# A perceiver layer on one core: GpSimd takes nine of the low halves, the first pass ends in finer steps, and feature products change place

## The reference, cut to what matters

```python
Sim = (encoder_hc @ w1)[:, :, None] + (decoder_hq @ w2)[:, None, :] \
    + jnp.einsum('bid,bjd->bij', encoder_hc * w3, decoder_hq) + b_sim[0]
A = jax.nn.softmax(Sim, axis=2)
hq_hat = jnp.einsum('bij,bjd->bid', A, decoder_hq)
Batt = jax.nn.softmax(jnp.max(Sim, axis=2), axis=1)
hc_bar = jnp.einsum('bi,bid->bd', Batt, encoder_hc)[:, None, :]
hc_hat = jnp.broadcast_to(hc_bar, encoder_hc.shape)
feats = jnp.concatenate([encoder_hc, hq_hat, encoder_hc * hq_hat, encoder_hc * hc_hat], axis=-1)
hcq = feats @ W_qv + b_qv
```

## Time and profile before

| | us |
|---|---|
| three runs, median (lowest to highest) | 124.64 (123.28 to 125.08) |
| the profiled execution, device time | 122.58 |
| its span in the profile | 120.7 |
| first pass, first scores to last scores on PE | 6.3 to 43.3 |
| first exponential | 45.1 |
| first mix to last mix | 48.4 to 97.2 |
| tail | 97.2 to 120.7 |
| DMA traffic | 29.27 MB, at about 410 GB/s until 72 us |

### The profile page before, as it was taken

How to read it: one execution, slowest core, us unless ns; L and a number is a source line. 1 busy time by engine, 2 the same in 40 slices (tenths; PEclk the granted TensorE clock), 3 DMA queues, 4 the chain that set the end, 5 groups by cost and what they waited for, 6 DMA issues and landing times.

```text
span 120.7 us, 1711 instructions
## 1 busy us (share of the span) xinstructions
PE 111.7 (93%) x569; PEld 84.6 (70%) x569; DVE 93.5 (77%) x140; ACT 69.0 (57%) x118; POOL 23.9 (20%) x35
## 2 busy tenths in 40 slices
PE   6789999999999995999999999999999969999890
PEld 2237675858685872888898879899898947665280
DVE  1549999999999989799999964899999533271442
ACT  4075758467473209997998844988887530221220
POOL 2100000000003420327755502353540001000100
PEclk9999999999999999999999999999999999999999
DMA  3999999999999999999999994300000000000001
GB/s 85 347 406 415 413 411 406 410 411 406 413 407 408 410 414 404 411 413 433 385 414 407 408 334 181 87 5 0 0 0 0 5 0 0 0 0 0 3 0 43
DMA packets 8073, 29.27 MB, mean 242 GB/s; under 512 B 1025, under 2 KB 1281, under 8 KB 7810
## 3 DMA queue, kind: packets, MB, share of 16 engines
q1 hardware_dynamic: 7920, 29.17, 61.6%
q10 hardware_dynamic: 146, 0.01, 0.1%
HBM read 29.04 MB, written 0.13 MB: 242 GB/s over the span
## 4 chain that ended last, share of the span: by engine, by line
PE 45%; DVE 22%; issue 18%; DMA 7%; SPq 3%; ACT 1%; POOLq 0%; POOL 0%; DVEq 0%; ACTq 0%
PE mixed_ps L679 18%; DVE neg_scores L488 12%; PE mixed_ps L681 9%; PE scores_ps L662 8%; DVE pair L467 7%; DMA raw<-keys_dram 7%; PE side_ps L694 3%; SPq L310 2%; PE scores_ps L804 1%; ACT pair L362 1%; PE scores_ps L623 1%; PE scores_ps L810 1%; PE scores_ps L687 1%; PE scores_ps L686 1%; PE scores_ps L684 1%
## 5 line engine op out<-in xcount | busy, mean ns | idle before, releaser
L467 DVE TENSOR_TENSOR pair<-raw,pair 128x1024 fp32r<-128x1024 f32 (+1 forms) x43 | 52.2, 1227 | 2.9 <-POOL pair L346 2.6
L362 ACT ACTIVATE pair<-raw 128x512 fp32r<-128x512 f32 (+1 forms) x43 | 34.7, 809 | 25.1 <-DMA raw<-keys_dram 14.2
L679 PE MATMUL mixed_ps<-pair,turned_high 128*128 128x512 f32 x92 | 35.3, 416 | 1.1 <-DVE turned_low L494 1.1
L346 POOL CAST pair<-raw 128x512 fp32r<-128x512 f32 x24 | 21.4, 893 | 65.0 <-DMA raw<-rows_dram 33.0
L681 PE MATMUL mixed_ps<-pair,turned_low 128*128 128x256 f32 x92 | 25.8, 281 | 0.0
L679 PEld LDWEIGHTS mixed_ps<-pair,turned_high 128*128 128x128 f32 x92 | 17.3, 188 | 4.7 <-DVE pair L467 1.3
L494 DVE TENSOR_TENSOR turned_low<-scores_ps,turned_high 128x512 fp32r<-128x512 f32 (+1 forms) x25 | 16.8, 673 | 1.6 <-ACT turned_high L381 1.0
L681 PEld LDWEIGHTS mixed_ps<-pair,turned_low 128*128 128x128 f32 x92 | 17.4, 190 | 0.0
L373 ACT ACTIVATE neg_scores<-neg_scores,neg_max 128x1024 f32<-128x1024 f32 (+2 forms) x14 | 14.4, 1032 | 4.4 <-DVE neg_scores L488 4.4
L488 DVE TENSOR_SCALAR_CACHE_REDUCE neg_scores<-scores_ps,neg_max 128x1024 f32<-128x1024 f32 (+1 forms) x13 | 15.8, 1217 | 0.2
L662 PE MATMUL scores_ps<-ident,neg_scores 128*128 128x128 f32 x98 | 14.7, 273 | 0.3 <-ACT neg_scores L373 0.3
(11 more groups left out here) (126 smaller groups left out, 87.8 us busy)
## 6 DMA issues: line engine op xcount, KB each, us to landing
raw<-keys_dram SPq DMA_DIRECT2D x24, 512.0 KB, 9.0
raw<-rows_dram SPq DMA_DIRECT2D x24, 512.0 KB, 7.3
w<-weights_dram SPq DMA_DIRECT2D x1, 1792.0 KB, 9.0
w<-weights_dram SPq DMA_DIRECT2D x1, 1024.0 KB, 7.8
const<-const_dram SPq DMA_DIRECT2D x1, 320.0 KB, 9.3
raw<-keys_last_dram SPq DMA_DIRECT2D x1, 256.0 KB, 7.4
raw<-rows_last_dram SPq DMA_DIRECT2D x1, 256.0 KB, 2.7
x_sb<-x_dram SPq DMA_DIRECT2D x1, 128.0 KB, 2.1
```

The lines of the kernel that those rows point to most:

```text
L346: nc.gpsimd.tensor_copy(out=pair[:, use % PAIR_BUFS, 0, 2 * D:4 * D], in_=raw[:, slot(item), 2 * D:4 * D])\
L362: nc.scalar.activation(pair[:, use % PAIR_BUFS, 0, 0:columns], raw[:, slot(item), 0:columns], ACT.Copy)\
L467: nc.vector.tensor_tensor(out=pair[:, use % PAIR_BUFS, 1, 0:columns], in0=raw[:, slot(item), 0:columns], in1=pair[:, use % PAIR_BUFS, 0, 0 ...
L679: nc.tensor.matmul(mixed_ps[:, :].rearrange("p (h d) -> p h d", h=2), probs_high, both[:, :, t * D:(t + 1) * D], start=(k == 0 and t == 0) ...
```

## The change

- Native key chunks are now 0, 2, 6, 12 and 24 (five, one of them the short one), so 20 key chunks are split.
- POOL makes the low halves of key chunks 8, 10, 13, 15, 17, 19, 21 and of rows chunks 0 and 1, each one subtraction 128x1024 with two inputs in SBUF. DVE makes the others. POOL no longer makes half of the highs of rows chunks 0, 1 and 2; ACT makes these whole, ahead of the exponentials.
- `pair` has 6 uses for 4; `raw` has 8 slots for 10. Several tiles of the tail now lie in the space of `neg_scores` to make room.
- Chunks 22, 23 and 24 are evicted one by one (512, 512 and 256 columns). The exponentials and the splitting of chunk 0 come in two halves of 256 columns.
- `w_qv` is loaded behind rows chunk 1. The bias and `features(0)` are made between the passes, in place of the six dummy matmuls; `features(3)` is made behind the last mix, one half ahead of the turn of `hq` and one behind it.

```diff
-RING = 10
-PAIR_BUFS = 4
+RING = 8
+PAIR_BUFS = 6
+NATIVE_CHUNKS = (0, 2, 6, 12, 24)
+POOL_CHUNKS = (8, 10, 13, 15, 17, 19, 21)
...
-        return k % 4 == 0
+        return k in NATIVE_CHUNKS
...
+    pool_low_uses = [split_before[k] for k in POOL_CHUNKS] + [KEY_SPLITS, KEY_SPLITS + 1]
...
+    WHOLE_HIGHS = 3
...
+    evictions = [(k, k + 1) for k in range(0, CHUNKS - 3, 2)] + [(k,) for k in range(CHUNKS - 3, CHUNKS)]
...
+    exp_columns = [(0, CHUNK // 2), (CHUNK // 2, CHUNK), (CHUNK, 2 * CHUNK)] \
+        + [(k * CHUNK, min((k + 2) * CHUNK, S)) for k in range(2, CHUNKS, 2)]
...
+    parts = [(0, 0, 2), (0, 2, 4)] + [(k, 0, tiles_of(k)) for k in range(1, CHUNKS)]
...
-                if k == 5:
+                if k == 1:
                     sp.dma_start(w[:, 0:WB_Q, :], blocks_in[:, 0:WB_Q, :]).then_inc(w_qv_loaded, 16)
...
             power(0)
-            for k in range(FULL):
+            for use in pool_low_uses:
+                item = CHUNKS + use - KEY_SPLITS if use >= KEY_SPLITS else split_chunks[use]
+                pool.wait_ge(high_done, use + 1)
+                nc.gpsimd.tensor_tensor(out=pair[:, use % PAIR_BUFS, 1, :], in0=raw[:, slot(item), :],
+                                        in1=pair[:, use % PAIR_BUFS, 0, :].bitcast(F32), op=ALU.subtract)\
+                    .then_inc(pool_low_done, 1)
+            for k in range(WHOLE_HIGHS, FULL):
...
-            rows_high(0)
-            rows_high(1)
-            act.wait_ge(max_done, GROUPS + 1)
+            for k in range(WHOLE_HIGHS):
+                rows_high(k)
+            act.wait_ge(max_done, EVICTIONS + 1)
             exps(0)
             exps(1)
             probs_high(0)
             exps(2)
             probs_high(1)
-            rows_high(2)
+            exps(3)
+            probs_high(2)
             rows_high(3)
...
-            dve.wait_ge(hw1_done, 1)
-            dve.wait_ge(max_done, GROUPS + 1)
-            nc.vector.tensor_tensor(out=sim_max[:, :], in0=hw1_ps, in1=neg_max[:, GROUPS:GROUPS + 1],
-                                    op=ALU.subtract).then_inc(sim_max_done, 1)
-            rows_low(0)
-            rows_low(1)
+            rows_low(2)
             probs_low(0)
             probs_low(1)
...
-            keep_warm(WARM_MAX, mixed_ps[:, :])
+            add_bias(hcq_ps, BR_QV)
             turn_probs(0)
             turn_probs(1)
+            pe.wait_ge(w_qv_loaded, 16)
+            features(0, normed_t[:, 0, :, :])
+            turn_probs(2)
             mix(0)
...
                 if k == 10:
-                    pe.wait_ge(w_qv_loaded, 16)
-                    features(0, normed_t[:, 0, :, :], start=True)
-                    add_bias(hcq_ps, BR_QV, start=False)
                     nc.tensor.matmul(hcq_ps, ident[:, :], x_sb[:, :], start=False, stop=False)
-                    pe.wait_ge(hc_hat_done, DH)
-                    features(3, hc_hat_t)
                 mix(k)
 
+            pe.wait_ge(hc_hat_done, DH)
+            features(3, hc_hat_t, halves=[0])
             pe.wait_ge(hq_done, 1)
             turn_square(hq).then_inc(hq_turned, 1)
+            features(3, hc_hat_t, halves=[1])
```

153 lines of the change are left out of this document (87 added, 66 removed).

## The result

The changed kernel takes **126.76 us** (median of four executions, 125.23 to 129.16) where the kernel before, measured beside it, takes 124.23 (123.28 to 125.08). The ratio is 1.023, interval 1.017 to 1.029: slower, clear of no change, by 2.3% in the middle; whether by more than 2% the interval leaves open. Forecast was 123.1; the time lies inside the range of 119.8 to 127.0, but on the wrong side of no change.

The account below looks back on a forecast made before the run. TensorE and VectorE were both taken as full in the first pass, TensorE alone from the first mix. First pass +1.4, between passes -0.6, second pass -2.35 gave -1.55 us: 124.64 to 123.1 us, range 119.8 to 127.0.

Parts of the forecast that it names:

- The hold: First pass: time one GpSimd subtraction keeps VectorE's low half waiting, taken as 4 x 0.42 = 1.68 us from a copy.
- the bounds given, 0.84 and 2.44: First pass: the hold in us if both inputs were read at once, or if it were four whole copies.
- the point of 1.95: First pass: the hold in us from which the later first exponential eats the change's other gains.
- second rival: First pass: a long hold makes GpSimd's and VectorE's lows follow without a gap, so the change ends slower; chance 0.26.
- its 2.06: First pass: the hold in us by the Trainium skill's 4497 ns for 2048 columns; the second rival's case.
- full turns: First pass: nine GpSimd and eight VectorE lows without a gap; first exponential at 30.6 + 9 x hold; chance 0.26.
- The order of turns: End of first pass: one or two GpSimd lows ahead of chunk 23's low; first exponential at 45.2 or 47.8 us.
- The middle of two orders, +1.4: End of first pass: first exponential later by +0.1 or +2.7 us; no row told which, so +1.4 was taken.
- Between the passes, -0.6: First exponential to first mix: finer exponentials, high and transposes take 2.6 to 2.7 us against 3.28.
- third rival: Between the passes: ScalarE waits for a late load, or the clock falls to 1.2 GHz; 0 to 4 us; chance 0.08.
- The second pass, -2.35: Chunk 10: `features(0)` (0.87), the bias (0.62) and `features(3)` (0.86) leave TensorE's full queue, saving 2.35 us.
- the tail, 0: Behind the last mix: halves of `features(3)`, 0.43 us each, fit gaps of 0.65 and 0.47, costing 0.

Follow-up runs that it names:

- the run with one input: Changed kernel with a copy of `raw` in place of each of GpSimd's nine subtractions (those low halves wrong): 118.92 us, ratio 0.962 to the kernel before.
- the run with the low halves back: Changed kernel with GpSimd's nine low halves given back to VectorE and every fourth key chunk native as before: 120.21 us, ratio 0.968 to the kernel before.

## Why the prediction was wrong

- **The hold, the step that failed.** "I take 1.68" was one term, 4 x 0.42, and it measured 2.21. The reasoning, that GpSimd's reads cost alike whichever operation they are for, is refuted by the run with one input: 1.04 us for the copy of 1024 columns, 2.41 for the subtraction. The true value lies inside the bounds given, 0.84 and 2.44, but past the point of 1.95 that the second rival had named. The Trainium skill had the missing fact (GPSIMD Engine Reference, Elementwise — side-by-side cycle accounting): some 2.6 cycles an element with two inputs and 1.03 on the read path for a simple body. Their ratio of 2.5 would make the hold 0.42 x 2 (columns) x 2.5 (second input) = 2.1, an estimate; the prediction used only that page's total of 4497 ns, and gave its 2.06 the smaller chance.
- **The second rival is what happened.** It said first exponential = 30.6 + 9 x hold. With 2.22 that is 50.6; the traces show 50.73, 50.25, 50.30 and 50.07. Its sign for full turns ("TensorE waiting over 2 us in sum for low halves ahead of chunk 20") is met: 3.1 us by the weight loads, and 3.5 more at chunks 20, 22 and 23. From its formula the changed kernel is 50.6 - 45.1 - 2.95 = 2.5 us slower; at full clock it is 2.3. It had 0.26.
- **The order of turns.** The middle of two orders, +1.4, was no case that could happen. The worse came: both rows lows ahead of chunk 23's. Taken back, they give 3.2 us.
- **Between the passes, -0.6.** Right in mechanism and size: 2.66 to 2.68 us at full clock in three traces; where dummies stood in the way it was 2.94 to 3.34. The third rival came on top of it in the profiled execution; two more of the four had a dip somewhere, by their mean clock. "It never fell behind such a gap" was true of the trace before, whose gaps were shorter and had dummies ahead of them. The gap grew to 1.85 us and not to 1.3, because the late lows of chunks 22 and 23 push VectorE's last evictions behind TensorE's last scores. A gap of 1.3 would not have been safe either: other traces without dummies dip behind idle stretches of 0.66 to 1.13 us (last section). Price: 1.4 us in that execution (4.05 - 2.68), some 0.9 us of the median.
- **The second pass, -2.35, and the tail, 0.** Right; 49.53 to 47.18 us in the run that does this alone, and a gap of 0.22 us.
- **Loads.** The expectation for ten slots on the changed kernel took 39.95 us for the start of the high of rows chunk 0. It is that of rows chunk 1, as ScalarE's highs of rows chunks 0 and 1 show:

```profile
37.58 1.06 ACT L393 ACTIVATE pair<-raw 128x1024 fp32r<-128x1024 f32 x1 [0.88 <-PE scores_ps L687]
39.95 1.06 ACT L393 ACTIVATE pair<-raw 128x1024 fp32r<-128x1024 f32 x1 [1.31 <-DMA raw<-rows_dram]
```

  So rows chunk 0 was on time (37.4 forecast), and waited for TensorE to free a place in `pair`. The high of rows chunk 2 ended at 44.9 for 43.6, which costs nothing ahead of an exponential at 50.7. Without GpSimd's lows that margin is gone: there the third rival's wait did come, 46.16 in the run with the low halves back.

## What to carry to other kernels

Before work is shared between VectorE and GpSimd, count for each VectorE instruction how many inputs it reads from SBUF. Two of them, or a fast copy, take turns with GpSimd as whole instructions, so the moved work is hardly added capacity: the turn is held at GpSimd's slower pace (2.2 us for what costs VectorE 1.13). Here an eviction ran under each turn, and still VectorE made a round of two split chunks in 3.34 us, where two lows and an eviction of its own would take 2 x 1.13 + 1.21 = 3.47. That is 0.13 us gained for a whole low moved. One input at the usual pace, or an input in PSUM, leaves both free. And if the price of a hold is not in the trace, work out at what value the sign turns, and weigh the sides by that, not by the nearest row's multiple.
